# Attention by pairs of heads in all head-wise attentions, and four dense tiles moved into the end of the self attention

## The reference

```
x = rms_norm(hidden_states, ln_in_w)
mixed = where(vm, x @ v_qkv, x @ l_qkv);  q, k, v = split(mixed)   # 16 heads of 32
q, k = apply_rotary(q, k, position_ids, l)
ctx = sdpa(q, k, v, causal=True)                  # 112 queries x 112 keys
hidden = residual + where(vm, ctx @ v_dense, ctx @ l_dense)
cq = heads(rms_norm(hidden) @ cq_w);  ck, cv = split(encoder @ ckv_w)
cctx = sdpa(cq, ck, cv, causal=False)             # 16 heads of 16, 112 x 375
hidden = hidden + cctx @ cdense_w
```

## Time and profile before

| what | value |
|---|---|
| time of three runs | 2145.38, 2152.37, 2153.7 us, median 2152.37 |
| the profiled execution | 2153.12 us, its span 2151.3 us |
| TensorE matmul busy | 1999.6 us (93%) |
| TensorE weight loads busy | 1694.3 us (79%) |
| VectorE, ScalarE, GpSimd busy | 1179.8, 852.6, 887.9 us |
| mean granted clock of TensorE | 0.954 |

### The profile page before, as it was taken

How to read it: one execution, slowest core, us unless ns; L and a number is a source line. 1 busy time by engine, 2 the same in 40 slices (tenths; PEclk the granted TensorE clock), 3 DMA queues, 4 the chain that set the end, 5 groups by cost and what they waited for, 6 DMA issues and landing times.

```text
span 2151.3 us, 35629 instructions
## 1 busy us (share of the span) xinstructions
PE 1999.6 (93%) x12588; PEld 1694.3 (79%) x12588; DVE 1179.8 (55%) x3046; ACT 852.6 (40%) x2198; POOL 887.9 (41%) x1037
## 2 busy tenths in 40 slices
PE   4999897988889999999999999998878999998998
PEld 3865586766679999888888887996547888887898
DVE  6778766566555245354666645422165666664422
ACT  2026525565422112125666633322234666661321
POOL 3340302114048899974121126881043121103785
PEclk9999698897789999999999999999999999999999
DMA  3110100001013333331000022332131000001232
GB/s 120 40 55 2 45 8 15 9 21 50 3 43 105 117 108 114 122 103 36 14 20 12 12 83 69 108 108 75 67 102 42 9 18 12 22 2 40 88 109 83
DMA packets 38191, 118.87 MB, mean 55 GB/s; under 512 B 6169, under 2 KB 10265, under 8 KB 38017
## 3 DMA queue, kind: packets, MB, share of 16 engines
q1 hardware_dynamic: 31408, 107.92, 16.2%
q10 hardware_dynamic: 6608, 8.68, 1.4%
HBM read 114.75 MB, written 1.84 MB: 54 GB/s over the span
## 4 chain that ended last, share of the span: by engine, by line
PE 81%; DVE 9%; POOL 5%; issue 2%; ACT 2%; DMA 1%; DVEq 0%; SPq 0%; ACTq 0%; POOLq 0%
PE psum L544 15%; PE psum L545 13%; PE psum L546 13%; PE psum L755 8%; PE psum L766 7%; PE psum L809 6%; PE psum L537 4%; PE psum L660 4%; PE psum L662 4%; PE psum L661 4%; POOL wl L1603 3%; DVE rstd L1196 1%; DVE xc L1211 1%; POOL wh L1595 1%; PE psum L823 1%
## 5 line engine op out<-in xcount | busy, mean ns | idle before, releaser
L1603 POOL TENSOR_TENSOR wl<-raw,wh 128x256 fp32r<-128x256 f32 x656 | 517.7, 821 | 13.7
L1595 POOL TENSOR_SCALAR wh<-raw 128x1024 fp32r<-128x1024 f32 x164 | 183.7, 1120 | 459.5 <-PE psum L546 205.2
L544 PE MATMUL psum<-nh,wh 128*128 128x448 f32 x904 | 347.2, 384 | 14.5 <-DVEq L1379 7.8
L545 PE MATMUL psum<-nl,wh 128*128 128x448 f32 x904 | 336.9, 373 | 0.0
L546 PE MATMUL psum<-nh,wl 128*128 128x448 f32 x904 | 336.0, 372 | 0.0
L988 ACT ACTIVATE probs_t<-masked_t,nmin 112x375 f32<-112x375 f32 (+1 forms) x384 | 207.2, 540 | 129.8 <-DVE nmin L1314 113.3
L766 PE MATMUL psum<-cst,probs_t 112*125 112x112 f32 (+1 forms) x1304 | 240.5, 291 | 16.3 <-DVE probs_t L1325 16.2
L766 PEld LDWEIGHTS psum<-cst,probs_t 112*125 112x125 f32 (+1 forms) x1304 | 196.3, 194 | 59.0 <-DVE probs_t L1325 25.4
L1325 DVE TENSOR_SCALAR probs_t<-probs_t,rinv 112x376 f32<-112x376 f32 (+1 forms) x520 | 218.0, 419 | 18.5
L1451 DVE TENSOR_TENSOR hid_l<-scr,hid_h 128x448 fp32r<-128x448 f32 x108 | 94.1, 871 | 229.0 <-ACT hid_h L1063 228.4
L1314 DVE CUSTOM_DVE_ANT_0 masked_t<-psum,maskf 112x375 f32<-112x375 f32 x256 | 139.3, 545 | 124.4 <-PE psum L755 123.9
(11 more groups left out here) (178 smaller groups left out, 3854.8 us busy)
## 6 DMA issues: line engine op xcount, KB each, us to landing
raw<-in_walls SPq DMA_DIRECT2D x183, 512.0 KB, 3.5
raw<-in_ctxF SPq DMA_DIRECT2D x24, 375.0 KB, 3.0
ctxb<-in_ctxF ACTq DMA_DIRECT2D x8, 375.0 KB, 3.8
ctxt<-in_ctxK ACTq DMA_DIRECT2D x8, 375.0 KB
x<-in_xT ACTq DMA_DIRECT2D x2, 896.0 KB, 11.6
outT<-x SPq DMA_DIRECT2D x2, 896.0 KB, 5.8
mask<-in_kmask ACTq DMA_DIRECT2D x16, 41.0 KB, 2.6
vself<-in_tt SPq DMA_DIRECT2D x1, 448.0 KB, 6.8
```

Source lines behind the costliest of these rows:

```text
L544: nc.tensor.matmul(out, ah, bh, start=(i == 0), stop=False)
L545: nc.tensor.matmul(out, ah, bl, start=False, stop=False)
L1595: nc.gpsimd.tensor_scalar(high, src, 1.0, 1.0, ALU.mult, ALU.mult).then_inc(split_h, 1)
L1603: last = nc.gpsimd.tensor_tensor(low[cut], src[cut], high[cut].bitcast(F32), ALU.subtract)
```

## The change

Each attention except the memory attention now goes by pairs of heads on all engines: `a.pair` = 2. In one turn of the loop TensorE makes the scores of a pair, the projections that are due, both transposes of the pair two turns earlier (`LAG` now counts pairs), and the weighing of four heads whose transposes ended a turn before. ScalarE makes both exponentials, then copies. VectorE makes both minima, then for the pair before one reciprocal of two columns and both scalings. There are 6 buffers `probs` and 4 `masked_s`; the latter move to memory shared with `xc`, which is idle in the attentions. `att_c0` gets a mask of zeros and takes the fused operation and `masked_s` as the others do, so that its score banks come free when VectorE has read them. In `att_1` and `att_3` the two parts of a V tile are made two steps and one step later than before.

The four dense tiles of the first half of the tokens, in eight products of twelve matmuls, stand one to a pair in the last eight pairs of the self attention, which has no value projections there. The tiles of the second half and the norm that goes with them follow after the attention.

The diff, without the helper edits in `stage` that only select items:

```diff
@@ -55,7 +55,8 @@
 RING = 4
 BIG = 3.4028234663852886e38
 LAG = 2
-NPROB = 3
+NPROB = 6
+NMASK = 4
 NTURN = 5
 POOL = 3
 
@@ -286,14 +288,15 @@
         rinv = sb("rinv", [S, NPROB])
         eps = sb("eps", [P, 2])
         o_a = place[0]
-        masked_t = sb("masked_t", [S, 2, S2])
+        masked_t = at("masked_t", [S, NMASK, S2], F32, o_s + 2 * 4 * 8 * S)
+        assert 2 * 4 * 8 * S + 4 * NMASK * S2 <= o_n - o_s
         probs_t = sb("probs_t", [S, NPROB, 376])
         hid_h = at("hid_h", [P, 2, HALF], F32R, o_a)
         hid_l = at("hid_l", [P, 2, HALF], F32R, o_a + 8 * HALF)
         vtmp = at("vtmp", [S, 2, D], F32, o_s)
         assert place[0] <= 229344, place[0]
         vS = vself[0:S, :].rearrange("p (b d) -> p b d", b=B)
-        masked_s = [masked_t[:, i, :] for i in range(2)]
+        masked_s = [masked_t[:, i, :] for i in range(NMASK)]
         probs = [probs_t[:, i, :] for i in range(NPROB)]
         probsT = [probsT_t[:, i, :] for i in range(NTURN)]
 
@@ -498,10 +501,10 @@
 
             if not a.k_heads:
                 return []
-            first = {att_c0: -4}.get(a, -1)
-            second = {att_c0: -1}.get(a, 1)
+            first = {att_c0: -4}.get(a, 1)
+            second = {att_c0: -1}.get(a, 2)
             if s == -1:
-                return [("K", i, 0) for i in range(a.k_slots - 1)] + [("V", 0, 0)] + ([("V", 0, 1)] if second < 0 else [])
+                return [("K", i, 0) for i in range(a.k_slots - 1)] + ([("V", 0, 0), ("V", 0, 1)] if second < 0 else [])
             out = []
             if s % a.k_heads == 0:
                 out.append(("K", s // a.k_heads + a.k_slots - 1, 0))
@@ in stage() of TensorE @@
-            def stage(name, rhs_of, nblocks, who, mpc, ready=None, nn=None):
+            def stage(name, rhs_of, nblocks, who, mpc, ready=None, nn=None, items=None, only=None):
...
-                    for e in range(len(who)):
+                    for e in range(len(who)) if only is None else [only]:
@@ -737,7 +744,7 @@
                     return
                 if s >= 2:
 
-                    pe.wait_ge(a.maxed if a.mask else a.exped, s)
+                    pe.wait_ge(a.maxed, s)
                 wide = a.nk + a.nk % 2
                 passes = [(0, 0), (0, 1), (1, 0)] if a.k_heads else [(0, 0)]
                 for n, (i, j) in enumerate(passes):
@@ -830,19 +837,25 @@
                             chunk_last[(0, "v", c)] = (tile_ready, plan.n)
 
             def attention(a):
-                for s in range(a.steps + LAG + 2):
-                    if s < a.steps:
-                        if a is att_2 or s % 2 == 0:
-                            scores(a, s)
-                        for unit in projected(a, s):
-                            project(a, *unit)
-                        if a is att_self and s % 2 == 0 and s // NH + 1 < B:
-                            values(s // NH + 1, s % NH // 8, s % 8 // 2)
-                    if 0 <= s - LAG < a.steps:
-                        turn(a, s - LAG)
-                    w = s - LAG - 1
-                    if 0 <= w < a.steps and w % a.quad == a.quad - 1:
-                        weigh(a, w // a.quad)
+                pairs, wide = a.steps // a.pair, a.quad // a.pair
+                for n in range(pairs + LAG + 2):
+                    heads = range(a.pair * n, a.pair * n + a.pair)
+                    if n < pairs:
+                        scores(a, heads[0])
+                        for s in heads:
+                            for unit in projected(a, s):
+                                project(a, *unit)
+                            if a is att_self and s % 2 == 0 and s // NH + 1 < B:
+                                values(s // NH + 1, s % NH // 8, s % 8 // 2)
+                        if a is att_self and n >= pairs - 8:
+                            i = n - (pairs - 8)
+                            dense(items=[i // 2], only=i % 2)
+                    if 0 <= n - LAG < pairs:
+                        for s in heads:
+                            turn(a, s - LAG * a.pair)
+                    w = n - LAG - 1
+                    if 0 <= w < pairs and w % wide == wide - 1:
+                        weigh(a, w // wide)
 
             pe.wait_ge(cst_in, 16)
 
@@ -857,6 +870,11 @@
                                  start=True, stop=True).then_inc(tile_ready, 1)
 
 
+            def dense(items, only=None):
+
+                stage("dense", nhl, KD, ("dve", "dve"), 1, items=items, only=only,
+                      ready=lambda half, m: pe.wait_ge(att_self.out, att_self.steps // 8 * (half + 1)))
+
             stage("qk", nhl, KD, ("dve", "dve"), 1, nn=0)
             rotate(len(RAW) - 1)
 
@@ -868,8 +886,7 @@
             attention(att_self)
 
 
-            stage("dense", nhl, KD, ("dve", "dve"), 1,
-                  ready=lambda half, m: pe.wait_ge(att_self.out, att_self.steps // 4))
+            dense(items=range(4, len(SEQ["dense"])))
             for unit in projected(att_c0, -1):
                 project(att_c0, *unit)
             stage("cq", nhl, KD, ("dve",), 2, nn=1)
@@ -979,15 +996,18 @@
                 nc.scalar.copy(dst.rearrange("p c n -> p (c n)"), bank[0:KEYS, 0:w]).then_inc(emptied["act"], 1)
 
             def attention(a):
-                for s in range(a.steps + LAG):
-                    if s < a.steps:
+                pairs = a.steps // a.pair
+                for n in range(pairs + LAG):
+                    heads = range(a.pair * n, a.pair * n + a.pair)
+                    for s in heads if n < pairs else ():
                         act.wait_ge(a.maxed, s + 1)
                         if s >= NPROB:
                             act.wait_ge(a.turned, s - NPROB + 1)
-                        src = masked_s[s % 2][:, 0:a.nk] if a.mask else s_bank(s)[:, 0:a.nk]
+                        src = s_bank(s)[:, 0:a.nk] if a is att_2 else masked_s[s % NMASK][:, 0:a.nk]
                         nc.scalar.activation(probs[s % NPROB][:, 0:a.nk], src, ACT.Exp, scale=-1.0,
                                              bias=nmin[:, s % NPROB:s % NPROB + 1],
                                              accum_out=rsum[:, s % NPROB:s % NPROB + 1]).then_inc(a.exped, 1)
+                    for s in heads if n < pairs else ():
                         for unit in projected(a, s):
                             project(a, *unit)
                         if a is att_self and s % 8 == 7 and s // NH + 1 < B:
@@ -996,8 +1016,9 @@
                             context(a, s // NH + 2)
                         if a is att_2 and s + 2 < B:
                             context(a, s + 2)
-                    t = s - LAG
-                    if t >= 0 and t % a.group == a.group - 1:
+                    for t in range(heads[0] - LAG * a.pair, heads[0] - LAG * a.pair + a.pair):
+                        if t < 0 or t % a.group < a.group - 1:
+                            continue
                         g = t // a.group
                         act.wait_ge(a.turned, t + 1)
                         if g >= NTURN:
@@ -1290,49 +1313,62 @@
                 nc.vector.scalar_tensor_tensor(vS[:, b, :], bank[0:S, :], vmT[:, 1, b:b + 1], vtmp[:, b % 2, :],
                                                ALU.mult, ALU.add).then_inc(emptied["dve"], 1)
 
+            def smallest(a, s):
+
+                b, h = s // a.nh, s % a.nh
+                col = nmin[:, s % NPROB:s % NPROB + 1]
+                dve.wait_ge(a.scored, s + 1)
+                if s >= NMASK:
+                    dve.wait_ge(a.exped, s - NMASK + 1)
+                if a is att_2:
+                    nc.vector.tensor_reduce(col, s_bank(s)[:, 0:a.nk], AX_X, ALU.min).then_inc(a.maxed, 1)
+                    return
+                if a.mask == "keys" and h == 0:
+
+                    dve.wait_ge(a.mask_in[b % 2], 16 * (b // 2 + 1))
+                    nc.vector.tensor_scalar(maskf[:, b % 2, :], mask8[:, b % 2, :], -BIG, BIG,
+                                            ALU.mult, ALU.add).then_inc(a.masked, 1)
+                    dve.wait_ge(a.masked, b + 1)
+                m = {"causal": causal, "keys": maskf[:, b % 2, :], None: maskf[:, 0, :]}[a.mask]
+                nc.vector.tensor_tensor_reduce(out=masked_s[s % NMASK][:, 0:a.nk], in0=s_bank(s)[:, 0:a.nk],
+                                               in1=m, scale=1.0, scalar=BIG, op0=ALU.add, op1=ALU.min,
+                                               accum_out=col).then_inc(a.maxed, 1)
+
             def attention(a):
                 if a.nk == S2:
 
                     dve.wait_ge(chain, link(nc.vector.memset(probs_t[:, :, S2:S2 + 1], 0.0)))
-                wide = a.nk + a.nk % 2
-                for s in range(a.steps + LAG + 2):
-                    r = s - 1
...
+                if a is att_c0:
+
+                    dve.wait_ge(chain, link(nc.vector.memset(maskf[:, 0, :], 0.0)))
+                pairs, wide = a.steps // a.pair, a.nk + a.nk % 2
+                for n in range(pairs + LAG + 3):
```

(43 more changed lines are left out.)

50 lines of the change are left out of this document (13 added, 37 removed).

## The result

The changed kernel takes 2074.24 us (median of four runs, 2070.91 to 2077.38), the kernel before 2153.03 us in the same series: a ratio of 0.9638 with a 95% interval of 0.9608 to 0.9669. The prediction was 2081. The profiled execution took 2070.91 us, its span 2069.1, which is 82.2 less than the span before (2151.3).

What follows compares the result with a forecast made beforehand. TensorE's own work was taken to bound att_1 and att_3, waits and a low clock att_c0 and the self attention's end. Gains 50 + 6 + 12 + 3 = 71 off 2153.1 give 2082, median 2081; range 2058 to 2100 (0.65), on to 2122.

Steps and rivals of the forecast that it cites:

- att_c0, 50 predicted: att_c0: score banks freed at the second minimum, sixteen heads in 23.5 us, stage 197 for 247; bounds 28 and 55.
- To this I add 9 us of the 23.4 for the ends and a cold start: att_c0: 9 us added to eight times sixteen heads (188) for both ends and a cold start, making 197.
- the clock keeps falling: Rival, chance 0.17: clock falls for as large a share as now; att_c0 gains only 28, time 2112.
- only idle time comes back: Rival, chance 0.10: TensorE's busy time in att_c0 (215.70) stays; gain 31 less a tail of 3 there, time 2111.
- by it the gain would have been 54: att_c0: with weight loads at att_1's busy share of 89%, 193 us would be left, a gain of 54.
- Self attention, main part, 6 predicted: Self attention before its last eight pairs: fewer short waits for VectorE and low-clock turns; gain 6, between 2 and 10.
- which now has a reciprocal less per pair: Self attention, main part: VectorE saves one reciprocal per pair, 56 x 0.19 = 11 us.
- Last eight pairs and dense, 12 predicted: End of self attention with first half of dense: 30.8 us in place of 42.8, gain 12; 5 or 14 otherwise.
- att_1 and att_3, 3 predicted: att_1 and att_3: TensorE never idle, so only switches between kinds of matmul are saved; gain 3, from 0 to 12.
- Nothing shows that the new neighbours cost nothing, so I take 3: att_1 and att_3: two value-tile gaps saved per four heads give 12 us at most; 3 was taken.
- The rival of a new wait in this stage: Rival, chance 0.04, slower: in att_1 and att_3 ScalarE's V copy waits for a weighing and delays transposes; 83 us, time 2164.

Runs made afterwards that it cites:

- singles_late: Changed kernel with att_c0, att_1 and att_3 head by head, VectorE's low part of K tiles one head later, zero mask kept: 2095.36 us, ratio 0.9741.
- self_one: Changed kernel with all dense tiles as one block after the self attention, and the self attention head by head: 2091.08 us, ratio 0.9708.
- t_apart: Changed kernel with each value tile of att_1 and att_3 between the two transposes of its turn: 2074.85 us, ratio 0.9633.
- c0_one: Changed kernel with att_c0 head by head, its zero mask kept: 2093.46 us, ratio 0.9727.
- c0_both: Changed kernel with att_c0 head by head and without its zero mask: 2147.1 us, ratio 0.9972.
- cdense_in: Changed kernel with the four cdense tiles of the first half of the tokens in every second of att_c0's last eight pairs: 2060.18 us, ratio 0.9563.

## Why the prediction was right, and where its parts were not

The sign and the size were right: 2074 for 2081, with 82.2 us of gain in the profile where 71 were summed up. But three of the terms are off by 6 to 10 us each, not all to one side: 6.5 and 1.5 us too much for att_c0 and the dense tiles stand against 10.3 and 8.8 too little for the others. That the total is so near is in part luck.

*att_c0, 50 predicted, 43.5 measured.* The mechanism holds: scores wait for the second minimum, transposes 0.5 for the copies, and sixteen heads take 23.45 us (23.5 predicted). Inside that count two small misses cancel: four heads without a projection take 5.41 us and not 5.2, and the projections add 1.8 to four times that, not 2.7. Eight times 23.45 is 187.6; the stage takes 208.9. The step that failed is "To this I add 9 us of the 23.4 for the ends and a cold start": the 187.6 leave 21. From the last scores to cdense it is 11.4 us, 8.5 more than a pair takes, so the tail alone uses up the 9. The other 12.7 lie between first and last scores. There the clock is 0.74 in the first 20 us, and it isn't low at the start alone: it falls again at the end, where no projection fills the waits (0.84 and 0.77 in the rows above). This second fall comes in five of eight profiles; in the three without it first to last scores take 192.5 to 192.8 us and not 195.3 to 199.8. singles_late shows such an excess with another order: sixteen heads in 24.15 us, eight times that 193, and a stage of 208.9 already from first to last scores. The rival "the clock keeps falling" was thus true for a part of the stage, and false in its middle, where the clock is 1.00.

Before, TensorE was idle for 31 of 247 us of att_c0, and for 34 of the whole 252; after, 20.2 of 209 (209 less 188.78). So only some 13 of the 43.5 us are idle time, and the other 30 are busy time for the same work, at a clock of 0.92 in place of 0.82: the rival "only idle time comes back" is refuted, since busy time fell from 215.70 to 188.78 us. The Trainium skill, Perfetto Trace Analysis, section Identifying the Most-Contended Engine, prefers the busy share of weight loads as a measure of closeness to the limit; by it the gain would have been 54. It was nearer than the idle time (31) by 2 us only, and the share went to 155.13 of 209, 74%, and not to att_1's 89%.

*Self attention, main part, 6 predicted, 16.3 measured.* Outside its bounds of 2 to 10. The step "which now has a reciprocal less per pair" named the right engine but was not turned into time. Undoing the pairs alone costs 10.2 us of this part (100.8 against 90.6) at a clock of 1.00: 4.6 us by more idle time in its 99 us, and 28 times 0.12 to 0.14, some 3.6, by TensorE's own sequence; 2 us aren't placed. The other 6.1 (106.9 less 100.8) stand against a mean clock of 0.93 before, which self_one doesn't have although its self attention goes by the order of before; that low clock stands in the first 20 us (0.83, and 1.00 in self_one) and in the last 7 (237 to 244). Nothing shows that the change removed them.

*Last eight pairs and dense, 12 predicted, 10.5 measured.* Eight pairs with their twelve dense matmuls are full at a clock of 1.00, as predicted. What the working left out is what comes behind: the second half and the norm take 2.3 us longer. Undone as a block, 8 us come back up to att_c0 and 4 in the medians. This term is the least certain one.

*att_1 and att_3, 3 predicted, 11.8 measured.* The size is the bound of 12 that the prediction gave, and "Nothing shows that the new neighbours cost nothing, so I take 3" was the wrong choice. But the mechanism was wrong too, though the size of its bound was right: with the first gap of a value tile at 0.20 again (t_apart) the stage is 0.4 us longer and not 6. From the timelines, four heads before took 8.74 us: value tiles 1.51 behind a weighing (whose own 1.30 did not shrink) and 0.80 behind transposes, single transposes 0.41 ahead of scores or a weighing and 0.25 ahead of a value tile. What the pairs save is the value tile behind a weighing and one of the transposes that stood ahead of scores; that the sum (0.10 and 0.09) is the measured 0.18 is worked out from rows and not shown by a run of its own. The rival of a new wait in this stage is refuted: TensorE is busy 266.00 of 266 us.

What could have turned the sign was not in the list of rivals: the low part of the K tiles one head too early costs 19 us in each of att_1 and att_3, and with single heads in att_c0 14 us with the mask (c0_one against singles_late) and, if it is this alone that slows c0_both, 30 without (c0_both against before; no run without the mask has it at its old place). The new code has it there in pairs too. att_1 and att_3 lose nothing by it, since TensorE is never idle in them; for att_c0 no run shows what it costs in pairs.

## What to carry to other kernels

Count a turn from the timeline, but price a stage by asking where the turn leaves TensorE idle: here turns that were counted rightly made stages 15 to 21 us longer than the count, by the tail and by turns where TensorE idled some 0.4 us at a time and the clock was low. Independent matmuls of the next stage, dealt into such turns, cost nothing in att_c0 (cdense_in, 13 us faster); the first place to look is the end of a loop whose projections have run out. When an order is undone as an experiment, compare the undone stage with the stage before by its length: 291 against 272 us showed at once that something else had moved.

## What the runs showed of the hardware

The same att_c0, instruction for instruction, took 192.5 to 199.8 us from first to last scores in eight profiles of six kernels, by where the clock fell and rose. Differences under some 7 us in this stage tell nothing from one profile. The Trainium skill, TensorE: Matmul & The Clock Gate, section Part 1: The HAM clock gate, says that the number of matmuls at the low clock at the start of a kernel varies from run to run of one kernel. The traces here agree as far as two profiles of the changed kernel differ (197.9 and 195.3 us), but in the middle of a kernel and not at its start.

A matmul's visible gap isn't its cost: the same value tile started with a gap of 0.20 or 0.11 us, and the turns were 0.02 us apart, since a transpose took 0.25 us ahead of a value tile and 0.33 ahead of another transpose (0.74 for two, less 0.41 for a single one ahead of scores).
